# A graph-attention and expert kernel: four blocks of layer 1's products computed one stage earlier, and the slot table's one-hot rows made five blocks at a time

## The reference, cut to what matters

```python
def gat_layer(x, W, a_src, a_dst, bias, src, dst, heads, out_c, concat):
    h = (x @ W).reshape(n, heads, out_c)
    al_s = einsum('nhc,hc->nh', h, a_src); al_d = einsum('nhc,hc->nh', h, a_dst)
    e = leaky_relu(al_s[src] + al_d[dst], 0.2)
    ex = exp(e - segment_max(e, dst)[dst])
    alpha = ex / (segment_sum(ex, dst)[dst] + 1e-16)
    return segment_sum(h[src] * alpha[:, :, None], dst) + bias
h = elu(gat_layer(layernorm(x), W1, ..., heads=8, out_c=96))
x = x + gat_layer(h, W2, ..., heads=1, out_c=768)
logits = router(layernorm(x)); g, idx = top_k(logits, 2); gates = softmax(g)
W_up = w_fast + m_gate * w_slow + h_fast            # per expert, 768 x 192; W_down likewise
x = x + sum over the two experts e of gate_e * (square(relu(y @ W_up[e] + b1)) @ W_down[e] + b2)
```

## Time and profile before

| | us |
|---|---|
| median of 3 executions | 2488.86 |
| lowest, highest | 2483.84, 2489.70 |
| profiled execution, its own time | 2504.38 |
| its span, first to last instruction | 2502.5 |
| TensorE busy (matmul) | 1881.4 (75%) |
| VectorE busy | 1312.2 (52%) |
| ScalarE busy | 715.7 (29%) |
| GpSimd busy | 1263.7 (50%) |
| mean granted TensorE clock | 0.899 of 2.4 GHz |

### The profile page before, as it was taken

One profiled execution on the slowest core, in us unless ns is written; L12 is line 12 of the kernel. 1 busy time (PEld: TensorE's weight loads), 2 busy tenths in 40 slices (PEclk: granted clock), 3 DMA queues, 4 the chain that ended last, 5 costly groups with the idle time before them and its releaser, 6 DMA issues. The chain is left out here.

```text
span 2502.5 us, 32295 instructions
## 1 busy us (share of the span) xinstructions
PE 1881.4 (75%) x8856; PEld 1001.4 (40%) x8857; DVE 1312.2 (52%) x2900; ACT 715.7 (29%) x1721; POOL 1263.7 (50%) x1279
## 2 busy tenths in 40 slices
PE   1837887957777777756789867778777775899997
PEld 1325555522222222224445433333323323677775
DVE  7626667847676667658467412344343447522221
ACT  1514433211001101017223233443444440133332
POOL 5065553036666666632321135666666660277775
PEclk9968998979988999988889978888999996799999
DMA  5322321168888888889589597898998986388886
GB/s 177 114 59 56 100 62 43 54 201 288 289 285 291 287 285 292 281 274 277 154 220 265 124 295 268 314 319 305 316 311 310 323 306 235 84 139 139 138 138 104
DMA packets 171459, 533.04 MB, mean 213 GB/s; under 512 B 35105, under 2 KB 66060, under 8 KB 171122
## 3 DMA queue, kind: packets, MB, share of 16 engines
q0 software_dynamic: 99088, 379.24, 53.5%
q1 hardware_dynamic: 61490, 123.21, 14.1%
q10 hardware_dynamic: 10800, 29.70, 3.0%
HBM read 444.94 MB, written 87.10 MB: 213 GB/s over the span
## 5 line engine op out<-in xcount | busy, mean ns | idle before, releaser
L1502 PE MATMUL acc<-ring,work 128*64 128x388 f32 x880 | 208.2, 556 | 85.2 <-issue 61.3
L1796 PE MATMUL acc<-ring,work 128*64 128x384 f32 (+1 forms) x880 | 203.6, 570 | 80.4 <-issue 72.1
L920 PE MATMUL acc<-wg,work 128*128 128x384 f32 x600 | 224.7, 517 | 26.9 <-issue 17.7
L1640 POOL DMA_INDIRECT ring<-feat_tab,src_t x196 | 187.3, 955 | 109.4 <-PE acc L1796 46.6
L1907 ACT ACTIVATE work<-big,edges 128x64 f32<-128x64 f32 x392 | 135.9, 427 | 352.0 <-DMA edges<-in_w_slow 190.3
L1449 POOL DMA_INDIRECT ring<-feat_tab,src_t x196 | 185.3, 945 | 98.1 <-issue 47.6
L1253 PE MATMUL acc<-wg,work 128*128 128x384 f32 x600 | 217.8, 511 | 8.1 <-issue 6.3
L2109 POOL DMA_INDIRECT out_rows<-ring,wg x114 | 178.0, 1562 | 81.2 <-ACT ring L2206 60.0
L1754 DVE COPY work<-acc 64x384 f32<-64x384 f32 x100 | 56.0, 560 | 308.3 <-DMA edges<-in_w_scale 261.6
L1479 DVE TENSOR_TENSOR ring<-ring,mps 128x776 f32<-128x776 f32 x196 | 183.5, 959 | 56.9 <-DMA ring<-feat_tab,src_t 48.1
L869 POOL DMA_INDIRECT edges<-score_tab,src_p x152 | 147.4, 970 | 116.1 <-issue 45.2
(11 more groups left out here) (388 smaller groups left out, 3498.4 us busy)
## 6 DMA issues: line engine op xcount, KB each, us to landing
ring<-lo_rows SPq DMA_DIRECT2D x49, 256.0 KB
edges<-in_w_slow SPq DMA_DIRECT2D x28, 384.0 KB, 6.0
edges<-in_w_hebb POOLq DMA_DIRECT2D x28, 384.0 KB, 7.2
edges<-in_w_fast POOLq DMA_DIRECT2D x28, 384.0 KB, 8.6
unit_sum<-edges SPq DMA_DIRECT2D x28, 384.0 KB, 5.9
out_rows<-work SPq DMA_DIRECT2D x52, 192.0 KB
feat_tab<-work ACTq DMA_DIRECT2D x25, 388.0 KB
agg_raw<-work ACTq DMA_DIRECT2D x25, 388.0 KB
```

The source lines that it names most:

```text
L920: m = nc.tensor.matmul(acc[:, sl * 2 + c, 0:C // 2], xT[sl][:, k, :], wg[:, k, c * (C // 2):(c + 1) * (C // 2)], start=(k == 0), stop=(k = ...
L1502: m = nc.tensor.matmul(acc[c * WIN:(c + 1) * WIN, bank, 0:HALF], hot, row[:, c * HALF:(c + 1) * HALF], start=start, stop=True, skip_group_ ...
L1640: pool.indirect_dma_start(rows[k][:, 0:C], None, feat_tab[1], bass.IndirectOffsetOnAxis(ap=src_t[:, t:t + 1], axis=0)).then_inc(row_in[k], 16)
L1796: m = nc.tensor.matmul(acc[c * WIN:(c + 1) * WIN, bank, 0:n], hot, row[:, c * CHUNK:c * CHUNK + n], start=start, stop=True, skip_group_che ...
```

## The change

Features stage: the third pair of banks (acc 2:4) is taken from the transposes, which now wait for the ELU of block b - 2, and holds the products of blocks 0 to 3 with W1. They are made in sixteen pieces of three matmuls (`early_products`), one behind node_scores(b - 3) in each b from 6 to 21, straight from featT. ScalarE copies a finished block to work (`early_rows`, at b = 10, 14, 18, 22) and issues its store to feat_tab; the first piece of the next block waits for that copy.

Products stage: only blocks 4 to 24 are multiplied (NB1 = 21), 16 of them in the lookup loop and five behind it. The 20 units are spread over 21 blocks, not 25. The transposes of the edge weights and of the openings, and ScalarE's copies of them, come after the last block. The gather of the openings stands behind unit 20 and the exp's way through memory ahead of store 15.

Routing stage: VectorE makes the one-hot rows of five blocks (SB) of one choice with one operation on two tensors, the slot_hi comparison once and then two multiplications, in two places; ten turns with five matmuls each.

```diff
@@ -40,10 +40,13 @@
+SOON = 4
+SOON_AT = 6
+NB1 = NB - SOON
...
-STORES_BEFORE1 = 10
+STORES_BEFORE1 = 15
...
-OPEN_AT1 = 15
+OPEN_AT1 = 20
@@ -661,7 +664,9 @@
-            banks = [tps, acc[:, 0:2, :], acc[:, 2:4, :]]
+            banks = [tps, acc[:, 0:2, :]]
+            soon_row = [work[:, (3 + j) * C:(4 + j) * C] for j in range(SOON)]
+            soon_ps, soon_out, soon_st = (sem(n + L) for n in ("soon_ps", "soon_out", "soon_st"))
@@ -730,7 +735,7 @@
-                                               banks[b % 3][:, :, 0:3 * P].rearrange("p a (k n) -> p a k n", k=3),
+                                               banks[b % 2][:, :, 0:3 * P].rearrange("p a (k n) -> p a k n", k=3),
@@ -744,10 +749,10 @@
-                        if b >= 3:
-                            pe.wait_ge(h_ready, b - 2)
+                        if b >= 2:
+                            pe.wait_ge(h_ready, b - 1)
...
-                            m = nc.tensor.transpose(banks[b % 3][:, k // 3, (k % 3) * P:(k % 3 + 1) * P],
+                            m = nc.tensor.transpose(banks[b % 2][:, k // 3, (k % 3) * P:(k % 3 + 1) * P],
@@ -759,10 +764,27 @@
+                    def early_products(n):
+                        b, piece = n // 4, n % 4
+                        if piece == 0:
+                            pe.wait_ge(w_in, 16)
+                            pe.wait_ge(h_ready, b + 1)
+                            if b > 0:
+                                pe.wait_ge(soon_out, b)
+                        for at in range(piece * 3, piece * 3 + 3):
+                            k, c = at // 2, at % 2
+                            m = nc.tensor.matmul(acc[:, 2 + c, 0:C // 2], featT[:, k, b * P:(b + 1) * P], wg[:, k, c * (C // 2):(c + 1) * (C // 2)],
+                                                 start=(k == 0), stop=(k == KC - 1))
+                        if piece == 3:
+                            m.then_inc(soon_ps, 1)
...
+                        if 0 <= b - SOON_AT < 4 * SOON:
+                            early_products(b - SOON_AT)
@@ -776,7 +798,7 @@
-                        nc.scalar.activation(low[b % 3].rearrange("p (a n) -> p a n", a=2), banks[b % 3][:, :, 0:3 * P],
+                        nc.scalar.activation(low[b % 3].rearrange("p (a n) -> p a n", a=2), banks[b % 2][:, :, 0:3 * P],
@@ -792,6 +814,12 @@
+                    def early_rows(b):
+                        act.wait_ge(soon_ps, b + 1)
+                        nc.scalar.activation(soon_row[b].rearrange("p (a n) -> p a n", a=2), acc[:, 2:4, 0:C // 2], ACT.Copy).then_inc(soon_out, 1)
+                        act.wait_ge(soon_out, b + 1)
+                        act.dma_start(feat_tab[1][b * P:(b + 1) * P, :], soon_row[b]).then_inc(soon_st, 16)
@@ -800,11 +828,14 @@
+                        if b >= SOON_AT + 4 and (b - SOON_AT) % 4 == 0 and (b - SOON_AT) // 4 <= SOON:
+                            early_rows((b - SOON_AT) // 4 - 1)
...
+                    act.wait_ge(soon_st, 16 * SOON)
@@ -1212,7 +1243,7 @@
-                        if G >= SCAN_AT and (G - SCAN_AT) * LATE >= (stored + 1) * GPB1 * NB:
+                        if G >= SCAN_AT and (G - SCAN_AT) * LATE >= (stored + 1) * GPB1 * NB1:
@@ -1283,19 +1314,14 @@
-                             (LOOK_BLOCKS1 + 1, 3): lambda: carry_back(2, 1),
-                             (LOOK_BLOCKS1 + 5, 0): weights_out,
-                             (LOOK_BLOCKS1 + 6, 3): openings_out}
+                             (LOOK_BLOCKS1 + 1, 3): lambda: carry_back(2, 1)}
...
-                    for b in range(LOOK_BLOCKS1, LOOK_BLOCKS1 + 7):
+                    for b in range(LOOK_BLOCKS1, NB1):
...
-                    first = LOOK_BLOCKS1 + 7
-                    assert first % 2 == 1 and (NB - first) % 2 == 0
-                    with pe.Fori(0, (NB - first) // 2) as i:
-                        for j in range(2):
-                            products(i * 2 + (first + j), (first + j) % 2, lambda k: None)
+                    weights_out()
+                    openings_out()
@@ -1307,7 +1333,7 @@
-                        nc.scalar.activation(xT[sl], featT[:, :, ds(b * P, P)], ACT.Copy).then_inc(slot_ready, 1)
+                        nc.scalar.activation(xT[sl], featT[:, :, (b + SOON) * P:(b + SOON + 1) * P], ACT.Copy).then_inc(slot_ready, 1)
@@ -1316,7 +1342,7 @@
-                        act.dma_start(feat_tab[1][ds(b * P, P), :], raw[sl][:, 0:C]).then_inc(st_out[sl], 16)
+                        act.dma_start(feat_tab[1][(b + SOON) * P:(b + SOON + 1) * P, :], raw[sl][:, 0:C]).then_inc(st_out[sl], 16)
@@ -1327,25 +1353,23 @@
-                    for b in range(NB):
-                        if b + 1 < NB:
+                    for b in range(NB1):
+                        if b + 1 < NB1:
...
-                        while j < LATE and j * NB < (b + 1) * LATE:
+                        while j < LATE and j * NB1 < (b + 1) * LATE:
...
-                        if b == LOOK_BLOCKS1 + 5:
-                            act.wait_ge(exT_ps, 1)
-                            nc.scalar.activation(ex, tps[:, 0, 0:NT], ACT.Copy).then_inc(exT_ready, 1)
-                        if b == LOOK_BLOCKS1 + 6:
-                            act.wait_ge(open_ps, 1)
-                            nc.scalar.activation(ex_open[:, :], tps[:, 1, 0:NW], ACT.Copy).then_inc(exT_ready, 1)
+                    act.wait_ge(exT_ps, 1)
+                    nc.scalar.activation(ex, tps[:, 0, 0:NT], ACT.Copy).then_inc(exT_ready, 1)
+                    act.wait_ge(open_ps, 1)
+                    nc.scalar.activation(ex_open[:, :], tps[:, 1, 0:NW], ACT.Copy).then_inc(exT_ready, 1)
...
-                        act.wait_ge(st_out[sl], 16 + 16 * (NB // 2 + 1 - sl))
+                        act.wait_ge(st_out[sl], 16 + 16 * (NB1 // 2 + 1 - sl))
@@ -1939,7 +1963,9 @@
-            hot_lo, hot_hi = [xs(P) for _ in range(PLACES)], [xs(2 * TILES) for _ in range(PLACES)]
+            hot_lo = [xs(SB * P).rearrange("p (b n) -> p b n", b=SB) for _ in range(2)]
+            hot_hi = [xs(SB * 2 * TILES).rearrange("p (b n) -> p b n", b=SB) for _ in range(2)]
+            in_tile = [xs(SB * TILES).rearrange("p (b n) -> p b n", b=SB) for _ in range(2)]
@@ -1972,10 +1998,12 @@
-                    for n in range(TOP * NB):
+                    for n in range(TOP * NB // SB):
...
-                        nc.tensor.matmul(slots_ps, hot_lo[n % PLACES], hot_hi[n % PLACES], start=(n == 0),
-                                         stop=(n == TOP * NB - 1)).then_inc(place_used, 1)
+                        for j in range(SB):
+                            m = nc.tensor.matmul(slots_ps, hot_lo[n % 2][:, j, :], hot_hi[n % 2][:, j, :], start=(n == 0 and j == 0),
+                                                 stop=(n == TOP * NB // SB - 1 and j == SB - 1))
+                        m.then_inc(place_used, 1)
@@ -2044,15 +2072,18 @@
-                    for n in range(TOP * NB):
-                        b, c = n // TOP, n % TOP
-                        if n >= PLACES:
-                            dve.wait_ge(place_used, n - PLACES + 1)
-                        V.tensor_scalar(hot_lo[n % PLACES], iota_f[:, :], slot_lo[c][:, b:b + 1], None, ALU.is_equal)
-                        for j, value in enumerate((token, gate[c])):
-                            ins = V.tensor_scalar(hot_hi[n % PLACES][:, j * TILES:(j + 1) * TILES], iota_f[:, 0:TILES],
-                                                  slot_hi[c][:, b:b + 1], value[:, b:b + 1], ALU.is_equal, ALU.mult)
-                        ins.then_inc(place_ready, 1)
+                    for n in range(TOP * NB // SB):
+                        c, own = n % TOP, slice(n // TOP * SB, n // TOP * SB + SB)
+                        if n >= 2:
+                            dve.wait_ge(place_used, n - 1)
+                        across = lambda v, w: v[:, own].unsqueeze(2).to_broadcast([P, SB, w])
+                        st.step(V.tensor_tensor(in_tile[n % 2], iota_f[:, 0:TILES].unsqueeze(1).to_broadcast([P, SB, TILES]),
+                                                across(slot_hi[c], TILES), ALU.is_equal))
+                        V.tensor_tensor(hot_lo[n % 2], iota_f[:, :].unsqueeze(1).to_broadcast([P, SB, P]),
+                                        across(slot_lo[c], P), ALU.is_equal)
+                        V.tensor_tensor(hot_hi[n % 2][:, :, 0:TILES], in_tile[n % 2], across(token, TILES), ALU.mult)
+                        V.tensor_tensor(hot_hi[n % 2][:, :, TILES:2 * TILES], in_tile[n % 2], across(gate[c], TILES),
+                                        ALU.mult).then_inc(place_ready, 1)
@@ -2060,7 +2091,7 @@
-                    dve.wait_ge(place_used, TOP * NB)
+                    dve.wait_ge(place_used, TOP * NB // SB)
...

```

## The result

| | before | changed |
|---|---|---|
| median of 4 runs, us | 2489.3 (2483.8 to 2492.8) | 2470.3 (2465.8 to 2473.6) |
| ratio, 95% interval | | 0.9924 (0.990 to 0.9948) |
| the profiled execution, us (span) | 2504.4 (2502.5) | 2465.8 (2464.0) |

The account below looks back on a forecast made before the run. TensorE was taken to bound the products stage, VectorE the features and routing stages. Terms +17.3, -32 and -10 gave -24.7 us, 2504.4 to 2479.7 profiled, 2464 us as median; range 2452 to 2482.

Parts of the forecast that it names:

- Turns of 4.05 us: Features stage: TensorE bounds the sixteen blocks with a piece, 4.05 us each instead of 3.28, +12.3 us in all.
- The lost bank, +0.9 once: Features stage: without the third bank, transposes(6) waits for a later ELU and starts 0.9 us later, once.
- Three waits of 3.1, 1.6 and 1.6: Features stage: TensorE waits three times for ScalarE's copy before the next block's first piece, +6.3 us together.
- Given back at the end, -2.2: Features stage: the last blocks have no piece and TensorE runs faster there, giving back 2.2 us.
- TensorE's -31.7: Products stage: with four blocks taken out, TensorE ends its last block 31.7 us sooner.
- +2 for the additional units: Products stage: 16 units instead of 13 inside the lookup loop load the DMA engines, +2 us, from 0 to +8.
- Rival C: Products stage: DMA holds the lookup loop, 13.3 us per block instead of 9.1, whole change +28 us, 2517; chance 0.08.
- The three tails at 1444 to 1446: Products stage's end: products, weights and openings all finish at 1444 to 1446 us, so the stage ends 34 us sooner.
- Slot table: Routing stage: ten turns instead of 50 for the one-hot rows, VectorE 1.97 us per turn, -10 us.
- full-clock end of -11.7: Routing stage: with TensorE at full clock VectorE bounds the slot loop, which then gains 11.7 us.
- rival A: Slot loop runs at full clock, or ScalarE's copies come earlier: -26 to -33 us, 2456 to 2462; chance 0.20.
- the 15.5 us between the profiled execution and the median: Whole kernel: the profiled execution's 15.5 us above the median was assumed unchanged when forecasting the new median.

Follow-up runs that it names:

- e3: Kernel before with two PSUM bank pairs instead of three for the features-stage transposes, no products moved; ratio 1.0006, features stage 102.4 us.
- e4: Changed kernel with ScalarE's copy of finished products put ahead of the negatives of its turn; ratio 0.9860, features stage 113.8 us.
- e1: Kernel before with the slot table's change alone; ratio 0.9940, features 100.1 us, products 263.7 us, to the gather 44.5 us.
- e2: Changed kernel with the slot table's old loop of 50 turns; ratio 0.9947, features 118.8 us, products 236.9 us.
- e6: Changed kernel with SyncE issuing four of the five last stores before waiting for the exp's landing; ratio 0.9906, products stage 221.3 us.
- e9: Changed kernel with ScalarE's exp of the edge scores one block earlier; ratio 0.9886, products stage 233.2 us.
- e5: Changed kernel run again without an edit, on a faster chip; ratio 0.9903, features 120.5 us, products 222.1 us.
- e7: Changed kernel with the copy ahead of its turn and three blocks moved, not four, in pieces of two matmuls; ratio 0.9871, features stage 106.6 us.
- e8: Changed kernel with GpSimd's 25 scatters spread two by two between weight loads, read back at the lookup loop's end; ratio 0.9859, products stage 209.0 us.
- e12: Kernel before with the slot table's change and the scatters spread two by two, no products moved; ratio 0.9906, products stage 241.8 us.
- e10: Changed kernel with three blocks in pieces of two matmuls, copy ahead, scatters spread, exp one block earlier; ratio 0.9755, 2446.3 us.
- e11: Changed kernel with four blocks in pieces of three matmuls, copy ahead, scatters spread, exp one block earlier; ratio 0.9766.

## Why the prediction was right, and where it was not

The sign, the place of each gain and the total (-23.2 by stages against -24.7 on record, -19.0 by medians) were right. Point by point:

**Turns of 4.05 us.** 4.19: sixteen turns cost 14.6 instead of 12.3, against the mean of 3.28 of the earlier trace rows. I had taken no seam, and each turn lost 0.14. (VectorE's steady turn is 3.15; the mean holds the one late turn described at e3, which the longer stage swallows. The cost comes out the same, but the idle time of a steady turn is 1.0 us and not 1.17.) TensorE was the bound as said, 14.0 of 14 us busy.

**The lost bank, +0.9 once.** Transposes(6) starts 33.5 us into the stage and did 32.5 before: +1.0. e3 shows the cover.

**Three waits of 3.1, 1.6 and 1.6.** They were 2.54, 1.16 and 1.16, since ScalarE's operations overlap by some 0.1 each. What the step missed is the clock behind the first one, 1.6 to 1.7 us in four executions, this one among them, and nought in two. Together 6.5 for 6.3, by luck. In e4 both went.

**Given back at the end, -2.2.** -1.95. So 14.6 + 1.0 + 4.9 + 1.7 - 2.0 = 20.2 of the 20.4 measured.

**Products stage.** TensorE's -31.7 became -34.2 at the last copy, but 2.6 of that is the lookup loop's spread: 172.5 us from first to last lookup, 175.1 in the profile of before, and both values come with the old number of units (172.2 and 172.7 in e1 and e3) as with the new (174.9 in e2). Against e1 the last copy is 31.5 us sooner. So -31.7 was right, and the DMA engines, which I charged with +2 for the additional units, charged nothing. In 1310 to 1330 us their share is 1.04 and TensorE has 19.61 of 20 us busy. Rival C is out.

**The three tails at 1444 to 1446.** This is the step that failed, by 4 us. On the same scale (13.4 us on) the last w_fast came 3.7 us sooner than I placed it, but the tail behind the last products was 8.7 us where I had 4.7. I took the 3.1 us of before from the exp's start to the way back, from a stretch with a DMA share of 0.51; here it is 5.9 at 0.84, 2.8 of the 4 us. And STORES_BEFORE1 = 15, which I counted as a help, leaves five stores behind that wait: the stage ends 3.6 us behind the copy of the openings in the changed kernel and 2.4 in e6 and e9, so they have at most 1.3 us in it. e6, which issued four of them earlier, won 0.6 us of tail, and the runs with the exp further from the end had tails of 4.1 to 6.5. The -32.6 of the two profiles beside -32 is luck: like against like the stage won 30 us, +2 for DMA that did not come and 4 of tail that did.

**Slot table.** 0.46, 0.83, 0.45 and 0.45 us for the operations (0.455 and 0.825 taken), 1.97 per turn as worked out. -11.0 against -10 lies near the full-clock end of -11.7, since only the first turns ran at 1.2 GHz. The Trainium skill (TensorE: Matmul & The Clock Gate, "What's actually happening") says that the throttled clock is the default and activity releases it; the trace agrees, with 0.50 in the loop's first 4.4 us and 1.00 from 2103 on. This part of rival A happened. Its other part, earlier copies, did not.

**The median.** I took over the 15.5 us between the profiled execution and the median. The changed kernel's profiled execution was its fastest, so the untouched stages differ between the profiles by more than the change's error; only stages compare. Of the distance between -23.2 of stages and -19.0 of medians, 2.7 us are the lookup loop's spread; like against like the stages say -20.5, e5's medians -20.8. The -24.7 on record is 4.2 us too good beside that: 3.1 too little for the features stage (the turns, above all), 2 too much for the products stage (the tail, less the +2), 1 too little for the slot table.

## What to carry to other kernels

Work moved into another engine's shadow is free only up to the idle time of that turn, slower engine less faster one; cut the pieces to about that size (here 1.0 us is idle; pieces of 1.30 cost 6.6 us of stage in e7, those of 1.94 cost 13.8 in e4, both with one more bank lost) and stop there, since the rest is exchanged one for one. Put the copy that frees a buffer ahead of the turn's own work on its engine when the next user is the bound. When a stage gets shorter, cost its tail again with the company it will then have. Look at the largest single wait of the stage before moving anything: here spreading one burst of small scatters won as much as all the moved products did (13.1 us in e8, 12.2 in the change's two stages), and more than twice as much on a slower chip (27.7). And see what stands on a queue behind its wait: e5's low bits waited behind a read-back that nothing needed yet.

## What the runs showed of the hardware

A wait of 2.54 us in a TensorE that had been busy throughout was followed by a slowed piece in four executions (2.83 to 3.87 us) and by one at full speed in two (2.17), with the same program of the features stage in all six; where it came, the lower clock cost 1.6 to 1.7 us in all. Beside twenty-five indirect scatters in a burst from GpSimd, engines that had nothing to do with them stood still on the slower chips: ScalarE for 28.9 us in one piece, 22.8 of them beyond what its program waits for, and TensorE for up to 2.5 us between weight loads of one block ("issue"), while from 1245 to 1260 us the DMA engines' share was 0.19. On the faster chips the same burst held none of them so. Spread two by two, the scatters left no such wait on either (e8 and e12, e10 and e11). Why the burst does this is not shown. And the same program (before) took 2245 and 2509 us on different chips; the changed kernel's two profiles are 237 us apart, 226 of them in the stages that gather by edge, while the features stage took the same 120.4 and 120.5.
